# VectorE adds each tile's expert result from its PSUM bank, without ScalarE's copy, and its store is issued earlier

## What is computed

```python
x = x + attention(layernorm(x), Wq, Wk, Wv, Wo)
n = layernorm(x)
probs = softmax(n @ Wg)
top_w, top_i = top_k(probs, 2)
combine = sum(one_hot(top_i) * top_w / (sum(top_w) + 1e-8))
h = square(relu(einsum('td,edh->teh', n, W1)))
y = einsum('teh,ehd->ted', h, W2)
out = x + einsum('te,ted->td', combine, y)
```

## Time and profile before

| | |
|---|---|
| median of 3 runs | 279.1 us (278.1 to 279.32) |
| the profiled execution's own time | 280.09 us |
| its span in the trace | 278.2 us |
| TensorE busy | 267.4 us (96%) |
| GpSimd busy | 210.8 us (76%) |
| VectorE busy | 202.5 us (73%) |
| ScalarE busy | 184.9 us (66%) |

### The profile page before, as it was taken

The page is one execution under the profiler, slowest core; times in us unless marked ns, Lnnn a source line. Parts: engine busy times, 40 slices in busy tenths (PEclk is TensorE's granted clock), DMA queues, the critical chain, the costliest instruction groups (busy, mean ns, idle before and its releaser), DMA issues.

```text
span 278.2 us, 8908 instructions
## 1 busy us (share of the span) xinstructions
PE 267.4 (96%) x3614; PEld 209.3 (75%) x3614; DVE 202.5 (73%) x489; ACT 184.9 (66%) x306; POOL 210.8 (76%) x221
## 2 busy tenths in 40 slices
PE   7999979998999999999999999999999999999995
PEld 5565657677887788778887788778887788788883
DVE  2778348984959986595758866595857679898783
ACT  2566538919794588675794578675794677777871
POOL 2235885999999988987989878988889848744452
PEclk9999999999999999999999999999999999999999
DMA  7328255205250251413350250104320251144202
GB/s 220 130 64 272 75 153 155 75 4 154 78 151 5 79 190 39 115 53 112 108 152 4 80 185 12 73 5 146 123 75 2 80 174 33 64 154 117 72 0 75
DMA packets 13592, 26.85 MB, mean 97 GB/s; under 512 B 1136, under 2 KB 6512, under 8 KB 13552
## 3 DMA queue, kind: packets, MB, share of 16 engines
q1 hardware_dynamic: 13552, 26.30, 30.0%
HBM read 24.07 MB, written 2.23 MB: 95 GB/s over the span
## 4 chain that ended last, share of the span: by engine, by line
PE 68%; POOL 10%; issue 10%; DVE 5%; DMA 2%; ACT 2%; POOLq 1%; DVEq 0%
POOL act_lo L1134 9%; PE h_ps L346 8%; PE y_ps L367 7%; PE y_ps L361 7%; PE h_ps L348 7%; PE h_ps L347 7%; PE y_ps L362 7%; PE bank L501 4%; PE bank L435 2%; PE bank L513 2%; PE bank L523 2%; PE bank L465 2%; DVE act_s L766 2%; PE bank L486 2%; PE y_ps L325 1%
## 5 line engine op out<-in xcount | busy, mean ns | idle before, releaser
L1134 POOL TENSOR_TENSOR act_lo<-act_f,act_hi 128x512 fp32r<-128x512 f32 x112 | 144.0, 1309 | 39.8 <-ACT act_f L976 39.4
L766 DVE SCALAR_TENSOR_TENSOR act_s<-h_ps,scale 128x1024 f32<-128x1024 f32 x64 | 77.7, 1216 | 26.9 <-issue 14.7
L971 ACT ACTIVATE act_hi<-act_s 128x1024 fp32r<-128x1024 f32 x64 | 68.5, 1071 | 24.4 <-DVE act_s L766 24.2
L976 ACT ACTIVATE act_f<-act_s 128x1024 f32<-128x1024 f32 x64 | 67.8, 1060 | 1.0 <-POOL act_lo L1134 1.0
L346 PE MATMUL h_ps<-x_hi,w_lo 128*128 128x512 f32 x128 | 53.3, 416 | 2.1 <-DVE act_s L766 2.1
L361 PE MATMUL y_ps<-act_hi,w_lo 128*128 128x512 f32 x128 | 52.5, 410 | 0.0
L348 PE MATMUL h_ps<-x_hi,w_hi 128*128 128x512 f32 x128 | 50.7, 396 | 0.0
L362 PE MATMUL y_ps<-act_hi,w_hi 128*128 128x512 f32 x128 | 50.5, 394 | 0.0
L347 PE MATMUL h_ps<-x_lo,w_hi 128*128 128x512 f32 x128 | 50.5, 394 | 0.0
L367 PE MATMUL y_ps<-act_lo,w_hi 128*128 128x512 f32 x128 | 40.4, 397 | 1.0 <-POOL act_lo L1134 0.9
L346 PEld LDWEIGHTS h_ps<-x_hi,w_lo 128*128 128x128 f32 x128 | 24.1, 188 | 9.7 <-DVE act_s L766 2.9
(11 more groups left out here) (123 smaller groups left out, 384.6 us busy)
## 6 DMA issues: line engine op xcount, KB each, us to landing
scale<-scratch SPq DMA_DIRECT2D x32, 512.0 KB, 4.2
x_t_in<-x_tr SPq DMA_DIRECT2D x8, 256.0 KB, 4.9
x_all<-x SPq DMA_DIRECT2D x8, 256.0 KB, 4.8
out<-out_sb SPq DMA_DIRECT2D x8, 256.0 KB, 4.0
scale<-w SPq DMA_DIRECT2D x2, 256.0 KB, 4.5
scale<-w SPq DMA_DIRECT2D x1, 512.0 KB, 4.2
cst<-constants SPq DMA_DIRECT2D x1, 417.0 KB, 5.2
cst<-constants SPq DMA_DIRECT2D x1, 296.0 KB, 5.4
```

Of the source, the lines that this page charges most:

```text
L766: nc.vector.scalar_tensor_tensor(out=act_s[:, u % 2], in0=h_ps[:, u % 2], scalar=0.0, in1=scale[:, f % 2, e].unsqueeze(1).to_broadcast([P, ...
L971: nc.scalar.activation(act_hi[:, u % 4], act_s[:, u % 2], ACT.Square).then_inc(act_hi_ready, 1)
L976: nc.scalar.activation(act_f[:, u % 2], act_s[:, u % 2], ACT.Square).then_inc(act_f_ready, 1)
L1134: nc.gpsimd.tensor_tensor(act_lo[:, u % 4, n], act_f[:, u % 2, n], act_hi[:, u % 4, n].bitcast(F32), ALU.subtract).then_inc(pool_low_ready, 1)
```

## The change

The tile `y_t`, ScalarE's `copy_y` and the semaphore `y_t_ready` are gone. `add_experts(f - 1)` reads `y_ps` for every tile and waits for `y_done`; in VectorE's program it moves from the end of tile f to behind `scale_h(f, 2)` and `low(8f + 1)`. TensorE's `w2_product(8f)` waits for `out_ready`, which the add counts. In SyncE's program `store(f - 1)` moves ahead of the loads of x and of the next tile's routing weights.

```diff
@@ sync
             for f in range(TILES):
                 load_scale(f, 2)
                 load_scale(f, 3)
+                if f >= 1:
+                    store(f - 1)
                 if f + 4 < TILES:
                     load(f + 4)
                     load_transposed(f + 4)
...
                     load_scale(f + 1, 0)
                     load_scale(f + 1, 1)
-                if f >= 1:
-                    store(f - 1)
@@ tensor, w2_product
                 elif e == 0:
-                    pe.wait_ge(y_t_ready, f)
+                    pe.wait_ge(out_ready, f)
@@ vector
             def add_experts(f):
                 if f >= 1:
                     dve.wait_ge(out_stored, DMA * f)
-                if f < TILES - 1:
-                    dve.wait_ge(y_t_ready, f + 1)
-                else:
-                    dve.wait_ge(y_done, UNITS)
+                dve.wait_ge(y_done, EXPERTS * (f + 1))
                 dve.wait_ge(x_sum_ready, f + 1)
-                nc.vector.tensor_tensor(out_sb[:], y_t[:] if f < TILES - 1 else y_ps[:], x_sum[:, f % SUM_RING],
+                nc.vector.tensor_tensor(out_sb[:], y_ps[:], x_sum[:, f % SUM_RING],
                                         ALU.add).then_inc(out_ready, 1)
...
                     scale_h(f, 2)
                     low(u + 1)
+                    add_experts(f - 1)
                     if a < TILES:
                         decay_k(a)
...
                 scale_h(f, 7)
                 low(u + 6)
-                if f >= 1:
-                    add_experts(f - 1)
@@ scalar
-            def copy_y(f):
-                act.wait_ge(y_done, EXPERTS * (f + 1))
-                if f >= 1:
-                    act.wait_ge(out_ready, f)
-                nc.scalar.copy(y_t[:], y_ps[:]).then_inc(y_t_ready, 1)
...
                     square(u + 1)
-                    copy_y(f - 1)
                     if p < TILES:
                         exponentiate(p)
```

More of the change, by code:

```diff
@@ L136, in build @@
         w2_in = spare[:, EXPERTS * HIDDEN:2 * EXPERTS * HIDDEN].rearrange("p (n d) -> p n d", d=P)
-        y_t = sb("y_t", [P, TILE])
         out_sb = sb("out_sb", [P, TILE])
@@ L218, in build @@
         pool_low_ready, dve_low_ready = sem("pool_low_ready"), sem("dve_low_ready")
-        y_done, y_t_ready, out_ready, out_stored = sem("y_done"), sem("y_t_ready"), sem("out_ready"), sem("out_stored")
+        y_done, out_ready, out_stored = sem("y_done"), sem("out_ready"), sem("out_stored")
         NORM_STEPS = 2
```

## The result

The changed kernel takes 280.65 us (median of 20 runs, 279.36 to 283.32) against 278.85 us of the kernel before (median of 20 runs, 277.45 to 280.69): ratio 1.0065, 95% interval 1.0043 to 1.0087. It is slower, by 1.8 us. The profiled execution took 280.04 us, its span is 278.1 us.

What follows compares the result with a forecast made beforehand. The prediction took TensorE's products, busy without a gap from 64 to 274 us, as the bound. Terms 0 + 1.19 + 0.55 = 1.74 us on 279.1 us gave 280.8 us, 0.6% slower, range 279.4 to 282.0.

Steps and rivals of the forecast that it cites:

- What bounds the kernel: 64 to 274 us: TensorE's products are the path; freeing other engines wins nothing, each TensorE wait is paid in full.
- Tile 6, +1.19: TensorE waits for the add behind VectorE's low part: 1.09 us, plus 0.10 for the start after a wait.
- Tile 7, +0.55: TensorE waits for the add behind VectorE's low part: 0.45 us, plus 0.10 for the start.
- the second rival: VectorE's low part ahead of the add is shorter, tile 7's wait falls away: 279.8 to 280.3 us; chance 0.15.
- Tiles 1 to 5 at 0: The add ends before TensorE wants the bank, 1.6 us to spare in tile 2, so no cost in all five.
- The add at 0.69: VectorE's add takes 0.69 us reading the bank; from SBUF 0.68 at the median and 1.79 at most.
- The queues at 0: SyncE's store ahead of the loads of x may delay them 0.3 us; worth 0.
- The sum: Whole kernel: 0 + 1.19 + 0.55 = 1.74 us more, so 280.8 us, 0.6% slower.
- ScalarE's busy time to fall by 4.1 us: Sign in the changed kernel's profile: ScalarE loses 7 copies of 0.584 us, 4.1 us in all.
- The expected waits of 1.1 and 0.45 us: Sign in the profile: TensorE waits twice behind VectorE's add, near 235 and 258 us, none in tiles 1 to 5.
- the mechanisms that would have made it faster: Rival: ScalarE paces TensorE, its seven copies hold up squares; up to 4.1 us back, 275.0 us; chance 0.05.
- the waits were hidden: Rival: VectorE reaches the add 1.1 us sooner in tile 6, no time changes, 279.1 us; chance 0.12.

Runs made afterwards that it cites:

- the two kernels that separate the tiles: Changed kernel with copy, late add and late store put back in tiles 6 and 7 (0.9983 of before), or in tiles 1 to 5 (1.0037).
- the two other kernels with the same stretch: Changed kernel with copy, late add and late store back in tiles 1 to 5 (1.0037), or with only the store at its old place (1.0046).

## Why the prediction was right

- **What bounds the kernel.** Right: with TensorE busy without a gap from 64 to 274 us, 2.9 us less of ScalarE and 2.2 us less of VectorE won nothing, and each late start was paid in full (1.71 us in the stretch, 1.8 us in the medians). That removing the copy won nothing is shown by the stretch from tile 1 to tile 5, 126.40 us before and 126.43 after.
- **Tile 6, +1.19.** 1.07 late by the row, and 0.10 for the start (234.34 to 234.68 for the next product): 1.17.
- **Tile 7, +0.55.** 0.45 late and 0.10: 0.55. The low part ahead of the add was held up for as long as before (1.20 against 1.19), so the order of VectorE and GpSimd did not turn, as the second rival would have had it. In all four traces that keep this order of instructions, the low part ahead of the add took 0.67 to 0.68 us in tile 6 and 1.18 to 1.20 us in tile 7, and the stretch was 73.18 to 73.24 us. So at these two places the wide spread of the lows was no spread between runs but one between places.
- **Tiles 1 to 5 at 0.** Right, by 126.40 and 126.43 us and by the two kernels that separate the tiles.
- **The add at 0.69.** 676 to 691 ns in all eight, where from SBUF one took 1790. The median is 681 ns from the bank and 682 from SBUF, so the 10 ns that spoke against the bank were not there. By the Trainium skill's rule on SBUF inputs (SBUF — State Buffer, Who interferes with whom) an add with one input in a bank is left alone by GpSimd; the trace agrees. With the add ahead of `scale_h`, the add at 231.92 took 0.69 us beside GpSimd's low part of 231.68, and that one took its usual 1.30.
- **The queues at 0.** Right for the time. A size was off: the load of x that went at 110.03 before went at 108.86, in a tile that came 1.79 us earlier in this trace (TensorE wants the bank at 109.64 and not at 111.43), so 0.6 us later and not 0.3. No wait of TensorE came of it.
- **The sum.** 280.8 us predicted, 280.65 measured, 1.0065 against a forecast of 0.6%. That the times agree so closely is in part luck: the interval allows 1.2 to 2.4 us, the forecast started from 279.1 us where the 20 executions of before have a median of 278.85, and the two other kernels with the same stretch came out at 1.0037 and 1.0046. What bears the forecast out is the stretch, 1.71 us longer where 1.74 was forecast.
- **A sign to look for that was wrong.** I expected ScalarE's busy time to fall by 4.1 us. It fell by 2.9. Seven rows of 0.584 us are 4.1 us, but a row overlaps its neighbours: in tile 2 the copy began at 109.10, 0.10 before the row ahead of it ended, and the next row began at 109.56, 0.12 before the copy ended. Busy time counts such overlaps once, which leaves 0.36 us of this copy.
- **The expected waits of 1.1 and 0.45 us** are the late starts; the list of waits has them as 0.9 and 0.3, for the reason told with tile 6.

The rivals, in the end: none of the mechanisms that would have made it faster was there, and the waits were hidden in five tiles of seven. Two things differ in tiles 6 and 7: the attention's products no longer cover the add, and VectorE has a low part ahead of it. The low part makes the larger share of the loss: with the add ahead of it, tile 7 has no wait at all and 0.58 of the 1.71 us are left, in tile 6. How long the wait would be with the low part there but the attention's products too, no run shows.

## What to carry to other kernels

Freeing a buffer without a copy can cost more than the copy when the engine that frees it has a queue: ask what stands ahead of the new reader, and how much work the next writer has left. Look at the tiles at the end of the loop one by one, since the cover (here the attention's products) thins out there first, and since another engine's queue can be longer there (here VectorE's, by the low parts). A move of one line past the other work of the same engine is often the whole remedy: here the same add, ahead of `scale_h`, cost nothing.

## What the runs showed that was not expected

The twelve traces have spans of 275.2 to 279.7 us, and most of the difference that the edits don't explain arises in the first 75 us or so. `project_v` of tile 1 starts between 74.08 and 77.05 us (in the two traces of the changed kernel at 75.23 and 74.09), while from there to tile 5 all twelve take 126.33 to 126.44 us. Behind TensorE's last product ten of them have 3.2 to 3.3 us; the doubled add has 3.8, for its second add, and the kernel with the late store 3.9, where the last store took 2.7 us to land in place of 2.0. The widest pair is that of before and of the kernel with the copy back in tiles 6 and 7, although none of their instructions up to there differ:

```profile
77.05 1.09 PE L435 MATMUL bank<-w_center,x_t_in 128*128 128x136 f32 x8
```

```profile
74.08 1.09 PE L446 MATMUL bank<-w_center,x_t_in 128*128 128x136 f32 x8
```

SyncE's queue shows where it is built up. SyncE issues the first roots' store, goes on when it has landed, and then issues four loads of routing weights and a load of x. Before:

```profile
31.62 0.35 SPq L264 DMA_DIRECT2D scratch<-combine_t  x1
34.76 10.96 SPq L278 DMA_DIRECT2D scale<-scratch  x4
45.77 0.43 SPq L252 DMA_DIRECT2D x_all<-x  x1
```

and in the kernel with the copy back in tiles 6 and 7:

```profile
30.69 0.35 SPq L270 DMA_DIRECT2D scratch<-combine_t  x1
33.01 9.74 SPq L284 DMA_DIRECT2D scale<-scratch  x4
42.79 0.43 SPq L258 DMA_DIRECT2D x_all<-x  x1
```

The store is issued 0.93 us earlier, the next load follows it after 2.32 us in place of 3.14, and the four loads take 9.78 us up to the load of x in place of 11.01. Together that is 2.98 us at the load of x, as much as at `project_v` of tile 1 (2.97), so in this pair the whole difference is there by 46 us. What delays each of the three steps was not taken apart. From tile 5 on, kernels with the same order of instructions around these places agree within 0.06 us. An effect of 0.1 to 0.6% in such a kernel is seen in a stretch of the trace behind the start far sooner than in the times: a first ratio of 0.9963, with an interval that left out 1, became 1.0001 with the same kernel.
